# A two-layer contextual attention on one core: GpSimd makes the odd tile of each pair of sums for the paste, VectorE the even one

## The reference, cut to what matters

```python
f = b[:, :, ::RATE, ::RATE]
w, Hs, Ws = _extract_patches(f, KSIZE, STRIDE)          # 3 x 3 patches, 1600 of them
xf = w.reshape(B, L, C * KSIZE * KSIZE)
yi = jnp.einsum('bpd,bld->blp', xf, wn)                 # wn: patches over their norms
yi = yi * mm
yi = jax.nn.softmax(yi * SOFTMAX_SCALE, axis=1)
yi = yi * mm
patches = jnp.einsum('blp,bld->bpd', yi, raw_w.reshape(B, L, C * kernel * kernel))
...
out = out.at[:, :, u:u + (Hs - 1) * RATE + 1:RATE, v:v + (Ws - 1) * RATE + 1:RATE].add(Pc[:, :, u, v])
```

## Time and profile before

| what | value |
|---|---|
| three runs | 1370.94, 1367.72, 1367.48 us; median 1367.72 us |
| the profiled execution | 1372.19 us, of which the span of its instructions is 1370.4 us |
| busy in the span | TensorE 1194.4 us (87%), VectorE 1169.1 (85%), ScalarE 994.5 (73%), GpSimd 584.3 (43%) |
| mean granted clock of TensorE | 0.966 of full speed |
| DMA | 138.36 MB in 179175 packets, 39% of the 16 engines' span |

### The profile page before, as it was taken

One profiled execution on the slowest core, in us unless ns is written; L12 is line 12 of the kernel. 1 busy time (PEld: TensorE's weight loads), 2 busy tenths in 40 slices (PEclk: granted clock), 3 DMA queues, 4 the chain that ended last, 5 costly groups with the idle time before them and its releaser, 6 DMA issues.

```text
span 1370.4 us, 20011 instructions
## 1 busy us (share of the span) xinstructions
PE 1194.4 (87%) x4910; PEld 750.1 (55%) x4910; DVE 1169.1 (85%) x2315; ACT 994.5 (73%) x2881; POOL 584.3 (43%) x510
## 2 busy tenths in 40 slices
PE   4785988979888889989899899988899889897896
PEld 3555654656546655565556555566555655465443
DVE  4576999889998899879998899988998799988872
ACT  2888676886778868796768877787777967687331
POOL 1002543346442554336442464425643365334772
PEclk9887999999999999999999999999999999999898
DMA  5311344335353353443444353533534434432442
GB/s 80 44 36 46 100 120 110 89 94 138 89 128 87 99 129 97 115 104 100 124 107 98 96 137 96 126 84 97 137 91 114 111 94 115 106 85 83 136 141 55
DMA packets 179175, 138.36 MB, mean 101 GB/s; under 512 B 119602, under 2 KB 177010, under 8 KB 179058
## 3 DMA queue, kind: packets, MB, share of 16 engines
q1 hardware_dynamic: 178898, 136.57, 39.2%
q10 hardware_dynamic: 160, 0.50, 0.2%
HBM read 19.76 MB, written 13.11 MB: 24 GB/s over the span
## 4 chain that ended last, share of the span: by engine, by line
DVE 43%; PE 21%; issue 17%; ACT 14%; SPq 2%; DMA 2%; DVEq 1%; POOL 1%; ACTq 0%; POOLq 0%
PE psO L586 12%; DVE S L1039 10%; DVE G L1102 9%; DVE Z L1126 8%; PE psG L534 6%; DVE G L999 6%; ACT S L808 5%; DVE G L994 3%; ACT G L727 2%; ACT G L819 2%; PE psG L549 1%; DVE Z L1123 1%; DVE Z L1122 1%; DMA SH<-G 1%; SPq L388 1%
## 5 line engine op out<-in xcount | busy, mean ns | idle before, releaser
L1243 POOL TENSOR_TENSOR G<-G,SH 123x492 f32<-123x492 f32 (+1 forms) x448 | 548.1, 1232 | 768.9 <-DMA SH<-G 766.3
L586 PE MATMUL psO<-Z,B 123*128 123x492 f32 (+2 forms) x1792 | 720.8, 533 | 73.8 <-DVE Z L1126 61.0
L586 PEld LDWEIGHTS psO<-Z,B 123*128 123x128 f32 x1792 | 336.3, 195 | 291.1 <-issue 142.1
L1039 DVE CUSTOM_DVE_ANT_0 S<-G,RB 123x492 f32<-123x492 f32 (+1 forms) x448 | 346.1, 784 | 18.5 <-ACT G L727 18.1
L819 ACT ACTIVATE G<-G,nb 123x492 f32<-123x492 f32 (+1 forms) x448 | 268.3, 642 | 128.5 <-DVE G L1102 126.9
L808 ACT ACTIVATE S<-S,nm 123x480 f32<-123x480 f32 (+3 forms) x560 | 309.1, 554 | 7.1
L534 PE MATMUL psG<-LH,HL 128*123 128x492 f16 (+2 forms) x1104 | 275.9, 359 | 32.0 <-ACT G L727 20.8
L1102 DVE SCALAR_TENSOR_TENSOR G<-G,RA,psB 123x492 f32<-123x492 f32 (+1 forms) x448 | 269.8, 644 | 0.4 <-PE psB L469 0.4
L1126 DVE TENSOR_TENSOR Z<-G 123x984 f32<-123x984 f32 (+2 forms) x192 | 230.5, 1200 | 29.3 <-POOL G L1243 27.6
L534 PEld LDWEIGHTS psG<-LH,HL 128*123 128x123 f16 x1104 | 144.4, 138 | 147.0 <-issue 64.8
L534 PE MATMUL psG<-H 128*123 128x492 f16 (+2 forms) x368 | 130.3, 354 | 0.0
(11 more groups left out here) (85 smaller groups left out, 748.0 us busy)
## 6 DMA issues: line engine op xcount, KB each, us to landing
SH<-G SPq DMA_DIRECT2D x336, 214.8 KB
SH<-G SPq DMA_DIRECT2D x112, 89.2 KB
SH<-G SPq DMA_DIRECT2D x336, 19.2 KB
XP<-x SPq DMA_DIRECT2D x20, 280.0 KB, 4.2
XP<-mid SPq DMA_DIRECT2D x20, 280.0 KB, 4.1
HL<-LH SPq DMA_DIRECT2D x16, 246.5 KB, 3.7
mid<-OSB SPq DMA_DIRECT2D x48, 80.0 KB, 2.4
out<-OSB SPq DMA_DIRECT2D x48, 80.0 KB, 2.3
```

The costliest lines, as they stand in the source:

```text
L586: last = pe.matmul(psO[:, b, 0:n], B[:, o:o + 128], Z[:, 2 * (s % 2) + j, 0:n], start=t == 0, stop=t == TILES - 1)
L1039: dve.tensor_tensor_reduce(S[:, slot, 0:n], G[:, g:g + n], RB[:, s0 * TW:s0 * TW + n], 1.0, 0.0, ALU.mult, ALU.max, mx[:, slot:slot + 1]). ...
L1243: pool.tensor_tensor(g, g, SH[:, o % SFREE, 0:n], ALU.add).then_inc(y1_made, 1)
```

## The change

`sum_pair` on VectorE becomes `sum_even`, which makes one tile of the pair, and a new `sum_odd` on GpSimd makes the other one. GpSimd does so at the head of its slot, ahead of `add_shifted`. A new semaphore `odd_z_made` counts the odd tiles. TensorE waits for it ahead of the second tile of a pair; ScalarE's `columns_free`, VectorE's `add_rows` and GpSimd's first `wrap` wait for both semaphores, which is one sequencer instruction more in each. The even sum waits for one addition of GpSimd less than the double sum did (2i + 2 in place of 2i + 3).

```diff
--- before.py
+++ after.py
@@ -238,6 +238,7 @@
         shj_in = sem("shj_in")
         y1_made = sem("y1_made")
         z_made = sem("z_made")
+        odd_z_made = sem("odd_z_made")
         z_used = sem("z_used")
         o_read = sem("o_read")
         stored = sem("stored")
@@ -581,6 +582,8 @@
                         pe.wait_ge(o_read, (u * NK + k + 1) * 2)
                     if k == 0:
                         pe.wait_ge(b_made, u * PAIRS + i + 1)
+                else:
+                    pe.wait_ge(odd_z_made, u * SLOTS + k * PAIRS + i + 1)
                 for b in range(2):
                     o = (2 * t + b) * 128
                     last = pe.matmul(psO[:, b, 0:n], B[:, o:o + 128], Z[:, 2 * (s % 2) + j, 0:n],
@@ -712,6 +715,8 @@
                     if k == 0:
                         act.wait_ge(wrap_made, u * PAIRS + min(t // 2 + 1 + t % 2, PAIRS))
                         act.sem_inc(act_gate, 1)
+                    act.wait_ge(odd_z_made, u * SLOTS + k * PAIRS + t // 2 + 1)
+                    act.sem_inc(act_gate, 1)
                     act.wait_ge(z_made, u * SLOTS + k * PAIRS + min(t // 2 + t % 2 + 1, PAIRS) + 1)
                     act.sem_inc(act_gate, 1)
 
@@ -982,6 +987,8 @@
                     if k == 0:
                         dve.wait_ge(wrap_made, u * PAIRS + min(t // 2 + 2, PAIRS))
                         dve.sem_inc(dve_gate, 1)
+                    dve.wait_ge(odd_z_made, u * SLOTS + k * PAIRS + t // 2 + 1)
+                    dve.sem_inc(dve_gate, 1)
                     dve.wait_ge(z_made, u * SLOTS + k * PAIRS + min(t // 2 + 2, PAIRS) + 1)
                     dve.sem_inc(dve_gate, 1)
                 if (j, "row2") in COPIED:
@@ -1103,11 +1110,11 @@
                                              in1=psB[0:TW, k % 2, 0:n],
                                              op0=ALU.mult, op1=ALU.subtract).then_inc(arg_made, 1)
 
-            def sum_pair(at, s):
+            def sum_even(at, s):
                 u, k, i = at
                 c0, n = z_cols(k)
                 slot = 2 * (s % 2)
-                dve.wait_ge(y1_made, u * NB + k * TILES + min(2 * i + 3, TILES) + SFREE)
+                dve.wait_ge(y1_made, u * NB + k * TILES + 2 * i + 2 + SFREE)
                 dve.sem_inc(dve_gate, 1)
                 if k == NK - 1 and i == 0:
                     dve.wait_ge(wrap_made, (u + 1) * PAIRS)
@@ -1117,14 +1124,10 @@
                     dve.sem_inc(dve_gate, 1)
 
                 dve.wait_ge(z_used, u * SLOTS + k * PAIRS + i + 1)
-                g = G[:, :].rearrange("p (t c) -> p t c", c=GLEN)
-                if i == 0:
-                    dve.tensor_tensor(Z[:, slot, 0:n], g[:, 0, c0:c0 + n], SHJ[:, 0:n], ALU.add)
-                    dve.tensor_tensor(Z[:, slot + 1, 0:n], g[:, 1, c0:c0 + n], g[:, 0, c0 - TW:c0 - TW + n],
-                                      ALU.add).then_inc(z_made, 1)
-                else:
-                    dve.tensor_tensor(Z[:, slot:slot + 2, 0:n], g[:, 2 * i:2 * i + 2, c0:c0 + n],
-                                      g[:, 2 * i - 1:2 * i + 1, c0 - TW:c0 - TW + n], ALU.add).then_inc(z_made, 1)
+                tile = G[:, 2 * i * GLEN + c0:2 * i * GLEN + c0 + n]
+                above = (2 * i - 1) * GLEN + c0 - TW
+                dve.tensor_tensor(Z[:, slot, 0:n], tile, G[:, above:above + n] if i else SHJ[:, 0:n],
+                                  ALU.add).then_inc(z_made, 1)
 
             def body(u, v, w):
                 for s in BODY:
@@ -1134,7 +1137,7 @@
                         argument_pair(at)
                     at_z = place(u, v, s + 1)
                     if at_z:
-                        sum_pair(at_z, s + 1)
+                        sum_even(at_z, s + 1)
                     if s == 23 and v is not None:
                         lse_max(v, False)
                     if s == 24 and v is not None:
@@ -1227,6 +1230,8 @@
                 if i == 0 and not (isinstance(u, int) and u == 0):
                     pool.wait_ge(z_made, u * SLOTS + 1)
                     pool.sem_inc(pool_gate, 1)
+                    pool.wait_ge(odd_z_made, u * SLOTS)
+                    pool.sem_inc(pool_gate, 1)
                 pool.wait_ge(y1_made, u * NB + 2 * i + 2 + SFREE)
                 pool.sem_inc(pool_gate, 1)
                 g = G[:, :].rearrange("p (t c) -> p t c", c=GLEN)
@@ -1242,8 +1247,25 @@
                     g = G[:, t * GLEN + c0:t * GLEN + c0 + n]
                     pool.tensor_tensor(g, g, SH[:, o % SFREE, 0:n], ALU.add).then_inc(y1_made, 1)
 
+            def sum_odd(at, s):
+                u, k, i = at
+                c0, n = z_cols(k)
+                pool.wait_ge(y1_made, u * NB + k * TILES + min(2 * i + 3, TILES) + SFREE)
+                pool.sem_inc(pool_gate, 1)
+                if k == NK - 1 and i == 0:
+                    pool.wait_ge(wrap_made, (u + 1) * PAIRS)
+                    pool.sem_inc(pool_gate, 1)
+
+                pool.wait_ge(z_used, u * SLOTS + k * PAIRS + i + 1)
+                tile, above = (2 * i + 1) * GLEN + c0, 2 * i * GLEN + c0 - TW
+                pool.tensor_tensor(Z[:, 2 * (s % 2) + 1, 0:n], G[:, tile:tile + n], G[:, above:above + n],
+                                   ALU.add).then_inc(odd_z_made, 1)
+
             def body(u, v):
                 for s in BODY:
+                    at = place(u, v, s + 1)
+                    if at:
+                        sum_odd(at, s + 1)
                     at = place(u, v, s + AHEAD)
                     if at:
                         add_shifted(at)
```

## The result

The changed kernel took 1355.65 us against 1369.33 us beside it, a ratio of 0.9897 with a 95% interval of 0.987 to 0.9924. That was four executions each, and it didn't hold at this size: run twice more on other chips the same kernel gave 0.9987 (0.9963 to 1.0011) and 0.9947 (0.9923 to 0.9971). Its 27 executions lie between 1350 and 1371 us with a mean of 1361.3, the 54 beside them of the kernel before between 1361 and 1373 with a mean of 1367.1. So the change is **faster by about 0.4%, 6 us**, where the forecast said slower by 0.8%; its range, 1347 to 1412, held all three medians. The size is less certain than each interval says: the first and the second don't overlap, and the second includes 1. Every ratio here leaves out slow executions, of which there was one, of y_behind, with 3648.49 us.

The account below looks back on a forecast made before the run. VectorE and TensorE were taken to pace each other, VectorE a little ahead. Path +3, doubled waits +2 and tail +6 made +11 us on the profiled 1372.2, so 1383, or 1379 against the median; range 1347 to 1412.

Parts of the forecast that it names:

- What leaves VectorE: VectorE's double sums: making only the even tile takes 103 us off VectorE, from lone durations.
- What GpSimd gets: GpSimd: 224 additions more, 241 us, which by itself fits in its idle time.
- What it costs VectorE: VectorE's two-SBUF-input operations: new waits for GpSimd's odd sums, 107 us, bounds 0 and 179.
- On the path: The chain: half of each VectorE term counts, 51 us leaving and 54 us coming, net +3 us.
- The delay of the additions behind the odd sum: GpSimd's queue: additions of pair s + 3 come later, costed at nothing, covered by 766 us idle ahead of DMAs.
- Doubled waits: Row additions and copies: one more sequencer instruction each, 105 on VectorE, 280 on ScalarE; +2 us, between 0 and 30.
- The tail: Last pastes, from 1270 us: GpSimd becomes the bound at 4.3 us a wide pair; +6 us, between 0 and 13.
- The rule of the full path: Port pair of VectorE and GpSimd: an exclusive lock for a whole instruction, against VectorE operations with two SBUF inputs.
- The rival built on it: Shared SBUF path, wide pairs: full path makes the kernel much slower, 1414 us; chance 0.15.
- the signs that I named: Profile: GpSimd 860 to 900 us busy, VectorE within 20 of 1169, L1039 880 ns or more, tail pastes 4 us a pair.
- My rival "faster": GpSimd's odd sums under VectorE's arguments or waits: each costs 0.15 us, giving 1342 us, up to 1360; chance 0.32.

Follow-up runs that it names:

- y_behind: Changed kernel with GpSimd making the odd sum behind the two additions of its slot, not ahead: 1394.69 us, 1.0182 of the kernel before.
- x_narrow: Changed kernel with GpSimd's odd sums cut to 8 columns from the second unit on: 1307.48 us, 0.9574 of the kernel before.
- x_twice: Changed kernel with each odd sum made twice on GpSimd, once into a scratch tile: 1442.9 us, 1.055 of the kernel before.
- x_memset: Changed kernel with GpSimd filling zeros for about as long in place of odd sums from the second unit on: 1321.12 us, 0.9664 of before.
- z_three: Changed kernel with three slots of Z in place of two: 1363.46 us, ratio 0.9967, with the changed kernel at 1365.73 us beside it.
- y_nogate: Changed kernel without the doubled wait in VectorE's row additions: ratio 0.9959.
- w_nogate: Changed kernel without the doubled wait in VectorE's row additions, run again beside the changed kernel on one chip: ratio 0.9977.
- x_split: Changed kernel with VectorE making both tiles in two instructions, even first, doubled waits kept, GpSimd making none: 1368.37 us, 1.0014 of before.
- z_three_old: The kernel before the change with three slots of Z in place of two: 1365.4 us, ratio 0.9982.

## Why the prediction was wrong

The balance was seen rightly, two large terms that nearly cancel, and the sign fell out of the sizes. **The step that failed is the cost to VectorE**, put at 107 us; the runs show 49 to 61. Put into the forecast's own sum, at a half on the path and with all else as it was, 61 gives -51 + 31 + 2 + 6 = -12 us, and so a faster kernel. By its steps:

- **What leaves VectorE, 103 us**: right. x_narrow, which leaves GpSimd almost only the instructions themselves, is 98 us under before, and the lone durations of VectorE's two-SBUF operations add up to 97 us less in the changed kernel.
- **What GpSimd gets, 241 us**: too much. The odd sum takes 1.05 us for 492 columns, not the 1.23 of the additions in place that it was priced by, and 0.76 at 328: some 206 us in all.
- **What it costs VectorE, 107 us**: this term failed, and with it the sign. Busy time fell by 41.5 us, so the new waits are 103 - 41.5 = 61 us, 0.27 for each odd sum; counted directly, 215 us of waits after 165, they are 49 us unrounded, 0.22 each. The rate that I took from the rows of before, 0.30 for each addition, would have given 67 us, near enough; the addition of more than half for a path that fills up was wrong. That it came near is in part luck: it left out L999 at 492 columns and the single sums, and all 165 us over 448 additions are 0.37 each, so the new sums cost less than the old additions. x_twice shows at a yet fuller path 95 us of busy time for 224 more, 0.42 each (0.38 counted directly), still under 107.
- **On the path, a half of each**: near for the work taken off (60 us of 98 in x_narrow), but too low for the new waits. From x_memset to the changed kernel VectorE's busy time rises by 51 us and the time by 40, four fifths. That and the next step are why of the 41.5 us some 6 arrive.
- **The delay of the additions behind the odd sum, costed at nothing**: wrong. GpSimd's occupancy without more waits of VectorE costs some 14 us (x_memset less x_narrow). The cover that I named, GpSimd's idle time ahead of DMAs, shrank from 766 to 393 us and was not gone, so idle time in the sum did not make the delay free. That the wait for the paste is a part of it was tried and not seen (z_three). Which of the queued operations costs the 14 us stays open.
- **Doubled waits, +2**: nothing measurable on VectorE (y_nogate, w_nogate), whose row additions are 17 a unit and not the 15 that I counted. ScalarE's 280 were never taken out alone; x_split holds them together with other changes.
- **The tail, +6**: about nothing. GpSimd is the bound there, as said, but at 3.8 us a pair and not 4.3:

```profile
1275.90 1.05 POOL L1261 TENSOR_TENSOR Z<-G 123x492 f32<-123x492 f32 x1
1276.91 2.84 POOL L1248 TENSOR_TENSOR G<-G,SH 123x492 f32<-123x492 f32 x2
1279.71 1.05 POOL L1261 TENSOR_TENSOR Z<-G 123x492 f32<-123x492 f32 x1
```

From 1275.90 to 1279.71 is 3.81 us: the odd sum's shorter time, and 0.4 us of waits in the two additions where I had 0.6. From the last unit's first paste to that of pair 203 it took 34.2 us before and 29.2, 32.0 and 31.5 after, but also 31.4 in z_three_old, where the double sum waits for one addition more as before; so that the even sum gains there is not shown. From the last unit's first paste to the end of the last one it took 108.3 us before and 105.8, 108.8 and 108.3 after.
- **The rule of the full path**: x_memset confirms what the Trainium skill's page "SBUF — State Buffer" says in "SBUF: two separate sides", that a GpSimd operation which reads SBUF and a VectorE operation with two SBUF inputs block each other: beside GpSimd's writes alone the maximum kept its 664 ns. The rival built on it was wrong in size, as the path didn't saturate.

Of the signs that I named, most moved as said, but less: GpSimd was busy for 796 us and not 860 to 900, the maximum of 492 columns took 860 ns and not 880, TensorE's pastes in the tail came at 3.7 us a pair (48.3 us for 13) and not 4; VectorE's busy time fell by 41.5 us where it was to stay within 20.

The account in time, from the runs: x_narrow's -60 us, +14 for occupancy, +40 for the reads, together the change's -6. These three are differences between neighbouring kernels and add up by construction; they divide the 6 us and don't confirm it. My rival "faster" had the right mechanism, a price below 0.4 us, but took 0.15 where it is 0.22 to 0.27, and its -26 us forgot the occupancy.

## What to carry to other kernels

Moving an elementwise sum with two SBUF inputs from a full VectorE to a GpSimd with room returned little here: of 60 us that leaving it out is worth, 54 were paid back, some 40 of them as VectorE's waits on the path that both read through. Before such a move, take the price for each operation from the groups (mean less lone duration, over all of them and not the largest alone, divided by the other engine's count), and don't raise it without a run that shows it; here it came out at 0.22 to 0.27 us where the groups of before said 0.30 to 0.37. Work of GpSimd that only writes SBUF was nearly free for VectorE here (x_memset), though not for the time, by some 14 us.

Put what another engine needs at the head of a slot (here worth 30 us), and don't time one operation into a cover without looking at what is queued behind it.

## What the runs showed that I had not expected

- The same GpSimd operation (two float32 inputs, 492 columns) takes 1.05 us for G and G and for the scratch tile and G, but 1.23 us for G and SH; at 369 columns the scratch tile and G in place take 0.96 us, G and G 0.83.
- Single executions of the changed kernel spread over 21 us, twice as widely as before (a standard deviation of 5.8 against 2.9 us; 4.6 and 4.7 inside the two larger sets). Four of them once agreed within 4 us and gave a ratio more than twice as far from 1 as the mean of all. VectorE's waits on the shared path don't explain it: they are 215, 214 and 216 us in three profiles of 1353.67, 1366.15 and 1365.34 us. What differs between these is TensorE's clock: it stood at the lower of its two levels, 1.2 GHz, for 85, 101 and 111 us in all, and its busy time was 1190.6, 1197.2 and 1201.0 us. Over the 27 executions time and mean granted clock (0.960 to 0.972) go against each other with a correlation of -0.75. Whether the clock makes an execution long, or both have one cause, no run separates.
